# The first attention's output projection in three passes over high and low halves

## The reference, cut to what matters

```python
x = x + tanh(g_xattn[0]) * cross_attention(layernorm(x), ctx, ...)     # 16 heads of 32: "A_" in the profile
x = x + tanh(g_ffn[0])   * mixture_of_depths(layernorm(x), ...)        # 256 chosen tokens a batch: "C_"
x = x + tanh(g_xattn[1]) * cross_attention(layernorm(x), ctx, ...)     # 16 heads of 64: "D_"
x = x + tanh(g_ffn[1])   * bit_linear_conv_ffn(layernorm(x), ...)      # "E_"

def cross_attention(x, y, Wq, bq, Wkv, bkv, Wo, bo):                   # the first one
    q = x @ Wq.T + bq ; k, v = split(y @ Wkv.T + bkv)                  # per head
    out = softmax(q @ k.T / sqrt(dh)) @ v                              # context of 128 rows
    return out @ Wo.T + bo                                             # the output projection that is changed
```

## Time and profile before

| | |
|---|---|
| median of 3 runs | 1800.57 us (1794.78 to 1801.24) |
| profiled execution | 1798.3 us, of it 1796.5 us span from first to last instruction |
| mean granted PE clock | 0.943 of full speed |
| PE busy | 1556.9 us (87%) |
| DVE busy | 1276.3 us (71%) |
| ACT busy | 883.3 us (49%) |
| POOL busy | 574.0 us (32%) |
| DMA | 142.34 MB, mean 79 GB/s |

### The profile page before, as it was taken

One profiled execution on the slowest core, in us unless ns is written; L12 is line 12 of the kernel. 1 busy time (PEld: TensorE's weight loads), 2 busy tenths in 40 slices (PEclk: granted clock), 3 DMA queues, 4 the chain that ended last, 5 costly groups with the idle time before them and its releaser, 6 DMA issues. The chain is left out here.

```text
span 1796.5 us, 25689 instructions
## 1 busy us (share of the span) xinstructions
PE 1556.9 (87%) x9559; PEld 948.6 (53%) x9559; DVE 1276.3 (71%) x2065; ACT 883.3 (49%) x1430; POOL 574.0 (32%) x556
## 2 busy tenths in 40 slices
PE   6798888987678889878999998999996878888886
PEld 4444444443355658645666665666664534444443
DVE  5576778888443546744777776767766699999995
ACT  4455555555444336435334343343332577777763
POOL 3132343233210012123112111220200497777770
PEclk9899999999788889989999999999999899999999
DMA  5112221222723434521020110201011411111111
GB/s 167 41 48 95 94 72 47 72 71 94 281 77 96 165 103 141 192 101 48 1 83 24 59 60 25 72 34 59 13 47 36 180 62 65 65 65 65 53 48 47
DMA packets 73284, 142.34 MB, mean 79 GB/s; under 512 B 8418, under 2 KB 17782, under 8 KB 72907
## 3 DMA queue, kind: packets, MB, share of 16 engines
q1 hardware_dynamic: 71914, 137.55, 22.2%
q0 software_dynamic: 960, 3.15, 0.6%
q10 hardware_dynamic: 288, 0.00, 0.0%
HBM read 97.67 MB, written 43.01 MB: 78 GB/s over the span
## 5 line engine op out<-in xcount | busy, mean ns | idle before, releaser
L2859 POOL TENSOR_TENSOR E_y<-E_y,E_centre 128x1024 f32<-128x1024 f32 x64 | 151.6, 2369 | 10.4 <-ACT E_y L2888 8.2
L2774 PE MATMUL E_OP<-E_w2q,E_yb 128*128 128x512 bf16 x512 | 128.3, 408 | 25.2 <-issue 18.9
L1454 ACT ACTIVATE D_oT<-D_OB 128x512 fp32r<-128x512 f32 x64 | 38.3, 598 | 219.5 <-DVE D_OB L1771 219.5
L2851 POOL TENSOR_SCALAR E_centre<-E_hs,E_cw,E_cb 128x512 f32<-128x512 f32 x64 | 106.9, 1670 | 59.7 <-DVE E_hs L2941 59.4
L2764 PE MATMUL E_HP<-E_xT,E_w1q 128*128 128x512 bf16 x512 | 123.3, 385 | 0.4 <-ACT E_xT L2865 0.2
L1743 DVE TENSOR_TENSOR D_q_low<-D_PJ,D_q_high 128x512 fp32r<-128x512 f32 x60 | 41.5, 691 | 98.7 <-ACT D_q_high L1430 98.7
L2950 DVE SCALAR_TENSOR_TENSOR E_y<-E_hs,E_cw,E_y 128x512 f32<-128x512 f32 x128 | 104.5, 855 | 1.1 <-POOL E_y L2859 1.1
L2774 PEld LDWEIGHTS E_OP<-E_w2q,E_yb 128*128 128x128 bf16 x512 | 52.1, 104 | 94.5 <-issue 47.2
L1523 PE MATMUL D_PJ<-D_xT_high,D_wq_high 128*128 128x512 f32 x240 | 101.7, 424 | 0.1
L588 PE MATMUL A_TX<-A_wo,A_oT 128*128 128x512 f32 x176 | 90.9, 642 | 7.1 <-PEq L1106 7.1
L1523 PE MATMUL D_PJ<-D_xT_high,D_wq_low 128*128 128x512 f32 x240 | 94.9, 395 | 0.0
(11 more groups left out here) (427 smaller groups left out, 4130.0 us busy)
## 6 DMA issues: line engine op xcount, KB each, us to landing
A_res<-in_x SPq DMA_DIRECT2D x8, 1024.0 KB, 5.3
xn_d<-A_xn SPq DMA_DIRECT2D x8, 1024.0 KB, 4.7
x_d<-A_res SPq DMA_DIRECT2D x8, 1024.0 KB, 5.9
W_raw<-in_w1T SPq DMA_DIRECT2D x16, 512.0 KB, 3.6
W_raw<-in_w2T SPq DMA_DIRECT2D x16, 512.0 KB, 3.9
D_res<-x_d SPq DMA_DIRECT2D x8, 1024.0 KB, 6.1
x_d<-D_res SPq DMA_DIRECT2D x8, 1024.0 KB, 4.4
E_res<-x_d SPq DMA_DIRECT2D x8, 1024.0 KB, 5.4
```

Source lines behind the costliest of these rows:

```text
L2774: mm = pe.matmul(OP[:, :], yb[:, k, c * P:(c + 1) * P], w2q[:, k, :], start=k == 0, stop=k == MC - 1)
L2851: pool.tensor_scalar(U[i % 2][:, 0, :], hs[i % NBUF][:, 0, 1:TILE + 1], cw[:, 2 * p, 1:2], cb[:, 2 * p:2 * p + 1], ALU.mult, ALU.add).then ...
L2859: pool.tensor_tensor(y, y, U[i % 2][:, :, :], ALU.add).then_inc(t0, 1)
```

## The change

The output projection is done as in the second attention. `divide` leaves its result in the PSUM bank `OB`; ACT copies it to float32r as the high half (`high_o`); DVE takes the rest as the low half (`low_o`), and that now raises the semaphore `o_ok` on which PE waits. The scaled weights are split the same way (ACT the high, POOL the low half, in step 0). `project_out` makes three passes (high x high, high x low, low x high) for each of the four k. On DVE `score` is moved ahead of `add_out`.

To find room the change also lays tensors over one another: the context's raw k over its low half (`kT`), the raw `wq` and `wo` over later tensors, the halves of the turned rows (`xT_halves`) over the place where the chosen tokens `xs` come to lie (so the gather also waits for the last q projection), the scratch `above` over the turned rows; `junk` and `later` become bfloat16. The core of the diff:

```diff
@@ project_out (PE)
             for k in range(part * QT // parts, (part + 1) * QT // parts):
-                mm = pe.matmul(out_bank(n, c), oT[n % 2][:, k, c * P:(c + 1) * P], wo[:, k, :],
-                               start=k == 0, stop=k == QT - 1)
+                for o, w in ((h, woh), (h, wol), (l, woh)):
+                    mm = pe.matmul(out_bank(n, c), o[:, k, c * P:(c + 1) * P], w[:, k, :],
+                                   start=k == 0 and o is h and w is woh, stop=k == QT - 1 and o is l)
@@ gather (POOL)
             pool.wait_ge(id_ok, 2 * (b + 1))
+            pool.wait_ge(q_mm, QT * STEPS)
@@ POOL, step 0
+            def low_wo(k):
+                pool.wait_ge(wo_hi, k + 1)
+                pool.tensor_tensor(wol[:, k, :], wo[:, k, :], woh[:, k, :].bitcast(F32), ALU.subtract).then_inc(wo_ok, 1)
@@ ACT
             def scale_wo(k):
-                act.activation(wo[:, k, :], wo[:, k, :], ACT.Copy, scale=tg).then_inc(wo_ok, 1)
+                act.activation(wo[:, k, :], wo[:, k, :], ACT.Copy, scale=tg).then_inc(wo_sc, 1)
+                act.wait_ge(wo_sc, k + 1)
+                act.activation(woh[:, k, :], wo[:, k, :], ACT.Copy).then_inc(wo_hi, 1)
+
+            def high_o(s):
+                act.wait_ge(o_div, s + 1)
+                act.activation(oh[s // GROUPS % 2][:, s % GROUPS, :], OB[:, :], ACT.Copy).then_inc(o_hi, 1)
...
                 if turn_x:
                     keep_xT(n + 2, 0)
+                high_o(s)
+                if turn_x:
                     keep_xT(n + 2, 1)
                 if s + 1 < SLOTS:
                     keep_mT(s + 1)
@@ DVE
             def divide(s):
                 dve.wait_ge(pv, s + 1)
-                dve.tensor_tensor(oT[s // GROUPS % 2][:, s % GROUPS, :], OB[:, :], rz[:, :], ALU.mult).then_inc(o_ok, 1)
+                dve.tensor_tensor(OB[:, :], OB[:, :], rz[:, :], ALU.mult).then_inc(o_div, 1)
+
+            def low_o(s):
+                dve.wait_ge(o_hi, s + 1)
+                dve.tensor_tensor(ol[s // GROUPS % 2][:, s % GROUPS, :], OB[:, :],
+                                  oh[s // GROUPS % 2][:, s % GROUPS, :].bitcast(F32), ALU.subtract).then_inc(o_ok, 1)
...
                 divide(s)
+                score(dve, s)
+                low_o(s)
                 add_out(dve, s)
-                score(dve, s)
```

More of the change, by code:

```diff
@@ L158, in context_tensors @@
     sb = lambda n, s, d: ctx.enter_context(nc.sbuf_tensor(L["name"] + n, s, d))
-    kh, kl = (sb(n, [P, L["inner"] // P, NB, CTX], F32R) for n in ("k_high", "k_low"))
-    return kh, kl, sb("V", [P, NB, L["inner"]], F32)
+    shape = [P, L["inner"] // P, NB, CTX]
+    kh = sb("k_high", shape, F32R)
+    with ExitStack() as over:
+        kT = over.enter_context(nc.sbuf_tensor(L["name"] + "kT", shape, F32))
+    return kh, sb("k_low", shape, F32R), sb("V", [P, NB, L["inner"]], F32), kT
 class ContextStage:
@@ L169, in __init__ @@
         self.io, self.L, self.banks = io, L, banks
-        self.kh, self.kl, self.V = kept_tensors
+        self.kh, self.kl, self.V, self.kT = kept_tensors
         self.cT, self.wk, self.wv = sb("ctxT", [P, KC, NB * CTX]), sb("wk", [P, KC, inner]), sb("wv", [P, KC, inner])
-        self.kT = sb("kT", [P, MT, NB, CTX])
         if L["bias"]:
@@ L342, in chosen_tensors @@
     sb = lambda n, s, d=F32: ctx.enter_context(nc.sbuf_tensor("S_" + n, s, d, side="right"))
-    return {"idx": sb("idx", [P, NB * HALVES], mybir.dt.uint32), "xs": sb("xs", [P, NB * HALVES, D]),
-            "base": sb("base", [P, NB * HALVES, D]), "got": ctx.enter_context(nc.semaphore("S_gathered"))}
+    with ExitStack() as over:
+        halves = [over.enter_context(nc.sbuf_tensor(f"A_xT_{n}", [P, KD, TILE], F32R, side="right")) for n in ("high", "low")]
+    return {"xs": sb("xs", [P, NB * HALVES, D]), "base": sb("base", [P, NB * HALVES, D]),
+            "idx": sb("idx", [P, NB * HALVES], mybir.dt.uint32), "xT_halves": halves,
+            "got": ctx.enter_context(nc.semaphore("S_gathered"))}
 def by_act(q):
@@ L370, in narrow_attention @@
         keep = lambda n, s, d=F32: ctx.enter_context(nc.sbuf_tensor(name + n, s, d, side="right"))
-        wo, wr = keep("wo", [P, QT, D]), keep("w_router", [P, D])
+        with ExitStack() as over:
+            wo = over.enter_context(nc.sbuf_tensor(name + "wo_raw", [P, QT, D], F32, side="right"))
+        wol, woh = keep("wo_low", [P, QT, D], F32R), keep("wo_high", [P, QT, D], F32R)
+        wr = keep("w_router", [P, D])
         R, N2 = ([keep(f"{n}{i}", [P, SUB, D]) for i in range(2)] for n in ("res", "xn2_"))
-        oT_last = keep("oT1", [P, QT, TILE])
-        junk = keep("junk", [P, D])
+        with ExitStack() as over:
+            wq = over.enter_context(nc.sbuf_tensor(name + "wq_raw", [P, KD, inner], F32, side="right"))
+        oT_last = keep("oT1", [P, 2, QT, TILE], F32R)
+        junk = keep("junk", [P, D], BF16)
         st2, mv2 = keep("stats2", [P, SUB, BN]), keep("mv2", [P, SUB, 2])
@@ L381, in narrow_attention @@
         upto, less, ties = keep("upto", [P, NC]), keep("less", [P, CHUNKS]), keep("ties", [P, CHUNKS])
-        later, lost = keep("later", [P, NB, NC, NC]), keep("lost", [P, NC])
+        later, lost = keep("later", [P, NB, NC, NC], BF16), keep("lost", [P, NC])
         rank = keep("rank", [P, NC])
@@ L385, in narrow_attention @@
         ties_at = keep("ties_at", [P, P], BF16)
-        kh, kl, V = context_tensors(nc, main, L)
+        context = context_tensors(nc, main, L)
+        kh, kl, V, _ = context
         wqh, wql = sb("wq_high", [P, KD, inner], F32R), sb("wq_low", [P, KD, inner], F32R)
@@ L389, in narrow_attention @@
         X = sb("x", [P, SUB, D])
-        xt = [sb(f"xT{i}", [P, KD, P]) for i in range(2)]
-        xh, xl = sb("xT_high", [P, KD, TILE], F32R), sb("xT_low", [P, KD, TILE], F32R)
+        with ExitStack() as over:
+            xt = [over.enter_context(nc.sbuf_tensor(f"{name}xT{i}", [P, KD, P], F32, side="right")) for i in range(2)]
+        above = keep("above", [P, S], BF16)
+        xh, xl = chosen["xT_halves"]
         qh, ql = sb("q_high", [P, QT, TILE], F32R), sb("q_low", [P, QT, TILE], F32R)
-        oT = [sb("oT0", [P, QT, TILE]), oT_last]
-        wq = oT_last[:, :, :].rearrange("p q n -> p (q n)").rearrange("p (k n) -> p k n", k=KD)
+        oT = [sb("oT0", [P, 2, QT, TILE], F32R), oT_last]
+        oh, ol = [o[:, 0, :, :] for o in oT], [o[:, 1, :, :] for o in oT]
         pr = sb("probs", [P, HG, TILE])
@@ L406, in narrow_attention @@
         with ExitStack() as early:
-            stage = ContextStage(nc, early, sem, io, L, (kh, kl, V), banks, side="right")
+            stage = ContextStage(nc, early, sem, io, L, context, banks, side="right")
         s_row = [sb("scores_row0", [P, S]), keep("scores_row1", [P, S])]
         lower = [keep(f"lower{i}", [P, S], BF16) for i in range(2)]
-        above, hot = keep("above", [P, S], BF16), keep("hot", [P, NC, CAP], BF16)
+        hot = keep("hot", [P, NC, CAP], BF16)
         PJ = ctx.enter_context(nc.psum_tensor(name + "PJ", [P, TILE], F32))
@@ L430, in narrow_attention @@
         stored = [sem(f"stored{i}") for i in range(2)]
-        wo_ok, bo_ok, m2z = sem("wo_scaled"), sem("bo_scaled"), sem("m2_zeroed")
+        wo_sc, wo_hi, wo_ok = sem("wo_scaled"), sem("wo_high"), sem("wo_low")
+        bo_ok, m2z = sem("bo_scaled"), sem("m2_zeroed")
         ln_st, ln_mv, ln_var, ln_rs, ln_x = (sem(n) for n in ("ln_stats", "ln_mv", "ln_var", "ln_rstd", "ln_x"))
@@ L437, in narrow_attention @@
         s_mm, s_ex = sem("s_made"), sem("probs_ready")
-        z_mm, pv, z_r, o_ok = sem("z_made"), sem("pv_made"), sem("rz_ready"), sem("oT_ready")
+        z_mm, pv, z_r, o_div, o_hi, o_ok = (sem(n) for n in (
+            "z_made", "pv_made", "rz_ready", "o_divided", "oT_high", "oT_ready"))
         z_ln, z_ex, z_t = sem("z_ln"), sem("rz_guess"), sem("z_times_guess")
@@ L714, in _ @@
                 sp.dma_start(X[:, c, :], x_dr[0, 0, :, c]).then_inc(first_in[c], 16)
-            sp.dma_start(wq, rows(io[L["wq"]])).then_inc(w_in, 16)
+            sp.dma_start(wq[:, :, :], rows(io[L["wq"]])).then_inc(w_in, 16)
             sp.dma_start(bq[:, :], io["bq0"]).then_inc(w_in, 16)
@@ L770, in _ @@
                 for c in range(SUB):
+                    if n == 0 and c:
+                        low_wo(c - 1)
                     if c == 1 and ahead:
@@ L785, in _ @@
                                 .then_inc(biased, 1)
+                    if n == 0 and c == SUB - 1:
+                        low_wo(c)
                     if n == STEPS - 1 and c == 1:
@@ L1187, in wide_attention @@
         keep = lambda n, s, d=F32: kept.enter_context(nc.sbuf_tensor(name + n, s, d, side="right"))
-        kh, kl, V = context
+        kh, kl, V, _ = context
         RING, OT = 2 * QG, QT // QG
```

1 line of the change is left out of this document (added).

## The result

The kernel after takes **1821.84 us** in the median of four runs (1818.54 to 1825.39), beside 1800.02 us for the kernel before in the same comparison: ratio **1.0127**, 95% interval 1.0095 to 1.016. Forecast were 1823 us and slower. The profiled execution of after took 1825.39 us, its span is 1823.6 us, the mean granted clock 0.933 (before: 1798.3, 1796.5, 0.943). One of the six executions of rows_first, further down, took 2885.25 us, is called slow, and is left out of its median and ratio.

The account below looks back on a forecast made before the run. PE was taken to bound the ordinary slot, DVE close behind; the new wait ahead of the maxima outweighs PE's gain. Terms sum to +19.9 us, with clock +23; on 1798.3 that is 1821, median 1823 us, range 1805 to 1838.

Parts of the forecast that it names:

- 1.85 us: Chain divide, high half, `mT`, scores: next scores start no earlier than 1.85 us after the start of divide.
- turning slots' 4.5: Slots that also turn and copy rows of x: scores start 4.5 us after divide, against 2.07 in slot 19 before.
- ordinary slots (7): Slots j = 1 of steps 1 to 6 and j = 2 of step 6: 0.55 to 1.05 us longer each, 5.5 together.
- j = 2 of steps 1 to 5: Third slots of these steps: four grow 0.05 to 0.5 us, slot 22 gains about 1.6; sum -0.6.
- turning slots (5): Turning slots of steps 1 to 5: 1.8 us more in slots 15 and 19, 0.5 in 7, 11 and 23; +5.2.
- j = 0 of steps 1 to 6: First slots of these steps, with the q projection: 0.6 to 1.0 us longer each before a small deduction; +4.3.
- slots 28 to 30: Step 7's three slots, distance from divide to scores just below the chain's: 0.1, 0.1 and 0.3 us; +0.5.
- last slot and block: Last loop slot and closing block, PE ahead and no wait for maxima: shorter passes gain, together -3.1 us.
- clock: PE's longer idling may halve its clock in five turning slots: 0 to 6.5 us, taken as +3.
- the rival with the clock: Clock falls in more places, also step 0 and j = 0 slots: +35 us, 1832 to 1838; chance 0.18.
- PE's busy time falls by about 30 us: Sign of being right: PE's busy time falls about 30 us while the layer ends some 20 later.
- The faster rival: If divide were ready early, slots would shrink with PE: 30 us less in full, 1770; chance 0.06.

Follow-up runs that it names:

- rows_first: Changed kernel with ACT's copies of the row and the sums moved ahead of the wait for the division; 1816.3 us, 1.009 of the kernel before.
- wait_only: Kernel before, only with ACT waiting for the division ahead of the copy of the turned maxima (second turned copy in turning slots); 1828.2 us, 1.0151.
- late_high: Changed kernel with the high half copied behind the maxima, row and sums; 1795.3 us, 0.9969 of the kernel before, and 0.9991 in a second comparison.
- wait_copy: As wait_only, plus a copy of the divided values into a spare tile behind the wait; 1825.9 us, 1.0152 of the kernel before.

## Why the prediction was right, and where it was not

**Right: the mechanism.** The high half on ACT stands ahead of `mT` and waits for the division, and PE's gain is lost in its own wait. wait_only makes two thirds of the loss without any work, and late_high keeps the work without the loss; beside it there is the clock, below. The 1.85 us were 1.87 in the first slots, the turning slots' 4.5 were 4.35 to 4.4 (4.6 in slot 3), and slot 0 lasted 12.98 where 12.9 stood.

**Luck: slot 19 and the total.** Slot 19 lasted 16.24 us where 16.0 stood, but with its scores and the first half of its q projection at half clock, which the 16.0 did not hold; in wait_copy and rows_first, with the same chain at a clock of 1.00 and 0.99, it lasted 15.0. Slot 15, at full clock, lasted 14.2 where 15.7 followed from the forecast. The median came within 1.2 us of 1823 because errors of both signs, each of several us, cancel, as the table shows. The table is of the slowest of the four executions of after, 3.5 us above the median.

**By the steps of the sum**, forecast and measured in the profiled executions (us):

| step | forecast | after | wait_only | late_high |
|---|---|---|---|---|
| slots 0 to 3 | +8.7 | +10.2 | +8.4 | +1.5 |
| ordinary slots (7) | +5.5 | +7.6 | +4.2 | -2.0 |
| j = 2 of steps 1 to 5 | -0.6 | -0.7 | +0.4 | +1.8 |
| turning slots (5) | +5.2 | +3.5 | +5.2 | -0.2 |
| j = 0 of steps 1 to 6 | +4.3 | +7.2 | +4.2 | +0.5 |
| slot 27 | -0.6 | -1.7 | -0.7 | -1.2 |
| slots 28 to 30 | +0.5 | +4.5 | +6.4 | +1.4 |
| last slot and block | -3.1 | -4.1 | -2.0 | -5.0 |
| clock | +3 | in the rows above | | |
| sum | +23 | +26.5 | +26.2 | -3.3 |

**The mis-sized term is the chain "1.85 us after the start of divide".** The scores also wait until the row and the sums of the ranking are copied out of their bank. Those copies stood behind `mT` with time to spare before, and came into the chain with it: 0.48 to the row's start, 0.16 to the sums', 0.34 to the scores, 2.20 in all. It is 0.33 us a slot from slot 8 on outside the turning slots, 0.44 in step 7, and rows_first takes it away: 6 to 7 us in all. The slots with j = 2 and 3 came out smaller than this would make them, because DVE's backlog shrank by more than I had counted: `divide` came 1.0 us sooner after the scores in slots 10, 14, 18 and 22 (11.80 to 10.78 in slot 14) and 2.0 sooner in slot 15, instead of 0.57.

**The clock was put in the wrong places.** The forecast had 3 us in the turning slots, on the six matmuls behind the maxima. There after shows full clock in all five (0.23 us from start to start in slot 19). The half clock cost more elsewhere: slot 1, where divide came 12.24 us after the scores instead of 11.27; slot 4, whose q projection ran at 0.43 us from start to start; and step 7. The first two are places that the rival with the clock had named, step 0 and the slots with j = 0; but its +35 did not come, and step 7 nobody had named. Windows of slot 4 in after and in before, clock 0.72 against 1.00:

```profile
100.00:115.80 15.80, 13.80 (x77) 8.28 (x76) 5.85 (x8) 7.42 (x13) 5.97 (x5) 0.72 0.38 134
```
```profile
90.00:102.20 12.20, 10.59 (x73) 5.27 (x72) 5.35 (x7) 6.30 (x11) 5.06 (x4) 1.00 0.52 173
```

In step 7 the clock was worth 3.0 us: slots 28 to 30 lasted 34.5 us, and 31.5 in wait_copy at full clock, whose scores start equally late behind the division. For slot 4 I count 12 x (0.43 - 0.233) = 2.4, for slot 1 the 1.0. With 6.7 us of the row and the sums that is 13.1 us that the sum did not hold, and the sum of the steps missed by 3.5. The 3 us of clock set for the turning slots did not come, and turning slots, slot 27 and block stayed 3.8 us below their terms. The remaining 2.8 us I have not separated.

**Wrong: "PE's busy time falls by about 30 us".** It stayed, 1556.3 against 1556.9 over the kernel. In slot 17 it fell by 0.52, from 10.96 to 10.44, not by 0.98. One reason is that the gain was sized too large. The forecast took 6 x 0.233 = 1.40 us for a half in three passes, but the first distance is 0.31 and from the last start to the next instruction 0.32: in late_high's slot 17 the second half takes 1.56 us, from 275.04 to the scores at 276.60, with no wait between. So three passes save 0.34 us a half there, not 0.49, and by my estimate from it some 22 us in 32 chunks, not 31. This error hardly shows in the sum, where the wait and not PE sets most slots. The other reason is how busy time is counted: the record of such a matmul lasts 0.39 to 0.48 us while the next one starts after 0.233, so that a stretch ahead of a wait counts as busy to the modelled end of its last record. And half clock lengthened other stretches. The start-to-start distances are the better measure of the passes.

**The faster rival.** "If divide were ready, the slots would shrink with PE: 30 less in full" was not in reach even without the wait. late_high removes the wait and gains 3 to 5 us, since half of each projection lies ahead of a wait for DVE's maxima, and the other half is shorter by 0.34 us.

## What to carry to other kernels

An instruction that waits puts all that is behind it on its in-order engine into its chain. Count everything queued there that anyone needs, not only the one that the reader has in mind: here `mT`, and behind it two small copies that gated the same matmuls. An added piece whose result is wanted late belongs behind those whose results are wanted soon, and that one move was worth 1.4 to 1.6% here. Shortening the busiest engine's work gives only what lies behind its last wait in a slot.

## What was not expected of the hardware

The granted clock of the same slots changed between variants that differ by half a microsecond a slot: the stretch of slots 28 to 30 had a mean clock of 0.80 in after and in wait_only, 1.00 in wait_copy and rows_first, and lasted 34 to 36 us or 30 to 31.5. In slot 29 of wait_only and of after PE had waited 2.14 and 2.11 us for the exponentials and ran at half clock behind it (8 matmuls 1.94 and 1.93 us); in rows_first it had waited 2.13 us at the same place and ran at full speed (1.06 us). So the length of the last wait alone, by which I had told the two cases apart at 2.48 and 3.00 us, does not decide it. What else does stays open here. The lines of after and then of rows_first:

```profile
450.50 1.12 PE L926 MATMUL A_SC<-A_k_high,A_q_high 32*128 32x128 f32 x16 [2.11 <-ACT A_probs L873]
451.55 1.93 PE L996 MATMUL A_ZB<-A_probs,ones 128*32 128x512 f32 x8
```
```profile
445.48 0.67 PE L926 MATMUL A_SC<-A_k_high,A_q_high 32*128 32x128 f32 x16 [2.13 <-ACT A_probs L873]
446.08 1.06 PE L996 MATMUL A_ZB<-A_probs,ones 128*32 128x512 f32 x8
```

In wait_only's slot 19 PE ran at half clock behind a stop of 1.97 us, shorter than the 2.48 us behind which it ran on at full clock before: the half of a projection took 3.51 us, where it takes 1.96 in the earlier trace rows.

```profile
317.78 0.73 PE L877 MATMUL A_TX<-ident,A_x 128*128 128x128 f32 x4 [1.97 <-ACT A_xT L794]
318.31 3.51 PE L588 MATMUL A_PJ<-A_wo,A_oT 128*128 128x512 f32 x4
```
